# Attention value product: key tails moved and stacked by DMA, loads in pieces, and a new order of the work

## The chip, the cores and the metric

One core of a Trainium2 chip runs the whole program. The metric is device time in microseconds (us), the median of the runs. TensorE (PE, with its weight loads shown as PEld), VectorE (DVE), ScalarE (ACT), GpSimd (POOL) and SyncE (SP, which here only issues DMAs) each run one queue of instructions in order and wait for each other by semaphores.

## What is computed

Cross attention followed by a soft mixture of experts. Two batches of 1024 rows attend with 16 heads of width 64 to a context of 154 rows; a head pair is 128 columns wide.

```python
x = x + attention(layernorm(x), ctx, ctx, mask)      # q = x Wq + bq, k = ctx Wk + bk, v = ctx Wv + bv
    s0 = where(mask, NEG, q k^T / sqrt(64)); p = softmax(s0)     # per head: 1024 x 154
    out = (p v) Wo + bo
x = x + ffn(layernorm(x))                            # 16 experts with 64 slots each
    se = layernorm(slot_embeds) * scale
    logits = x se^T                                  # 2048 x 1024
    dispatch = softmax(logits, over rows); combine = softmax(logits, over slots)
    slots = dispatch^T x
    eout = (gelu(slots Wg + bg) * (slots Wu + bu)) Wd + bd
    out = combine eout
```

## The kernel before, in words

**Two halves of every operand.** Each fp32 operand of a matrix product is split into a high half (rounded to fp32r, made by ACT) and a low half (the rest, made by DVE or POOL). A product of two operands takes three passes: high by high, high by low, low by high (`PASSES`).

**The attention loop.** The 2048 rows are 8 groups of 256 (two tiles, j = 0 and 1), and the 8 head pairs are 4 quads of two pairs (pp = 0 and 1). A step n is one group and one quad, so there are 32 steps, four to a group. The parts of a step are `Q` (query projection), `S` (scores), `R` (normalisation of the exponentials), `T` (transposes of the probabilities), `PV` (probabilities times values), and once a group `LN`, `XN`, `xT` (first norm and its transposes) and `Y` (output projection of a finished group, 24 matmuls for each tile). The loop is pipelined: what `STEP` lists for step n is `Q` of step n+1, `S` of n, `T` of n-1, `PV` of n-2. `Y` stands in the second step of a group.

**The tails.** 154 keys are 128 and 26 more. `T` of part 0 and 1 (`prob`, L1476) transposes the first 128 keys of a pair's two heads; `T` of part 2 (`prob_t`, L1479) transposes the 26-key tails of all four heads of the quad at once, 4 x 26 = 104 columns, into 104 partitions of one PSUM bank. ACT copies it to `pT_high` (L899) and DVE makes `pT_low` (L1155). A `PV` is three passes of two matmuls on the first 128 keys (L1499) and one on the tails (L1501), nine in all, each with 256 moving columns. The tail values `vt` are laid out for that block-diagonally by 8 DMAs from `tails` (L600), 4 for each batch.

**Queues.** PE runs `prologue + attention + logits + slots + experts + combine` in that order. DVE, ACT and POOL run the same list, each event shifted by a table (`LATER_DVE`, `LATER_ACT`, `LATER_POOL`). `EARLY` places the projections of keys (`K`), values (`V`, `VT`) and the splits of the weights between the first steps. PSUM is shared: 3 banks for scores (`NS`), 2 for transposes (`NT`), 3 for all else (`NA`); a bank is free when DVE has made the low half of what was in it. SP issues the loads in the order of `LOADS`, then the placements of the keys (`kbd<-keys`, two DMAs for each of 6 pairs, L607), `vt`, the second batch of x, `Wo` (L614), and later the slot embeddings (L617).

**The end of attention.** The slot embeddings are normalised on DVE (`SA` statistics, `SB` values) during steps 17 to 30, one a step, and transposed on PE (`seT`). The second norm of the rows, `N2`, is one DVE operation (L1213) and two on POOL (L752, L753) for each of 16 tiles, into a ring `x2f` of three buffers; `x2T` (L1534) transposes it, and `L` (L1552) makes the logits of a tile. `Ya` are parts of the last group's output projection that are done before its last `PV`. The first three `N2` stand behind the last `R` on POOL.

## Time and profile before

| | us |
|---|---|
| median of 3 runs | 544.6 (543.71 to 545.14) |
| the profiled execution, its own time | 544.24 |
| its span (first to last instruction) | 542.5 |
| PE busy | 530.0, 98% |
| DVE, ACT, POOL busy | 434.1, 402.2, 303.3 |
| attention, to the first logits | about 0 to 289 |
| logits, slots, experts, combination | about 289 to 542 |

In these tables a busy PE does not show how close it is to its limit, since matmuls overlap: a matmul of 256 columns is shown with some 284 ns, while the next one starts 120 ns after it. What PE work costs is read from the distance of starts.

### The profile page before, as it was taken

Reading aid. Unit: us, or ns where it says so; the run is one execution under the profiler, and the core shown is the slowest. Engines: PE = TensorE matmul, PEld = TensorE weight load, DVE = VectorE, ACT = ScalarE, POOL = GpSimd, SP = SyncE. Lnnn points to the kernel's source line nnn. Section 1 sums busy time; section 2 is a strip of 40 time slices with the busy share of each in tenths; the row PEclk is TensorE's granted clock in tenths of the full one; section 3 lists DMA queues with packets and bytes.
Section 4 is the critical chain, followed back from the end, with each engine's and each line's share of the span. In section 5 each row is a group of like instructions: output and inputs, shape, how many; then the busy total and the mean of one; then the engine's idle time right before and its main releaser. Section 6 shows DMA issues by size and latency. Waiting matters only on the chain.

```text
span 542.5 us, 11967 instructions
## 1 busy us (share of the span) xinstructions
PE 530.0 (98%) x3896; PEld 499.8 (92%) x3896; DVE 434.1 (80%) x1305; ACT 402.2 (74%) x1098; POOL 303.3 (56%) x327
## 2 busy tenths in 40 slices
PE   6999999999999999999998999999999999999997
PEld 4889999999999999999997888999978888899997
DVE  6777878787897979899677998798699888865453
ACT  5879969596896959779564555788979889766562
POOL 6674654544545455454365768787467999910000
DMA  8635000000030000000001333150288888525551
GB/s 257 181 86 179 3 1 2 2 2 1 3 98 2 2 2 1 2 0 4 0 1 80 155 156 156 78 201 1 79 264 283 270 306 288 182 79 170 181 167 67
DMA packets 34901, 54.11 MB, mean 100 GB/s; under 512 B 3997, under 2 KB 21497, under 8 KB 34713
## 3 DMA queue, kind: packets, MB, share of 16 engines
q1 hardware_dynamic: 34841, 53.36, 29.7%
q8 instruction: 32, 0.52, 0.4%
q14 instruction: 28, 0.23, 0.1%
HBM read 40.54 MB, written 10.49 MB: 94 GB/s over the span
## 4 chain that ended last, share of the span: by engine, by line
PE 90%; ACT 4%; DMA 2%; POOL 1%; DVE 1%; issue 1%; SPq 0%; ACTq 0%; DVEq 0%
PE ps L1461 9%; PE ps L1585 9%; PE ps L1357 9%; PE ps L1369 8%; PE ps L1610 8%; PE ps L1499 8%; PE ps L1439 7%; PE ps L1552 7%; PE ps L1476 5%; PE ps L1632 4%; PE ps L1501 4%; PE ps L1644 3%; DMA wvo_raw<-in_L_xattn_Wo_dram 2%; ACT expo L885 1%; PE ps L1615 1%; PE ps L1622 1%
## 5 line engine op out<-in xcount | busy, mean ns | idle before, releaser
L885 ACT ACTIVATE expo<-expo,nmin 128x154 f32<-128x154 f32 x256 | 106.2, 423 | 5.3 <-DVE nmin L1135 4.8
L1135 DVE CUSTOM_DVE_ANT_0 expo<-ps,maskb 128x154 f32<-128x154 f32 x256 | 69.1, 312 | 11.9 <-PE ps L1461 11.9
L723 POOL TENSOR_TENSOR prob_t<-expo,prec 128x104 f32<-128x104 f32 x64 | 23.1, 360 | 89.3 <-DVE prec L1146 89.1
L726 POOL TENSOR_TENSOR prob<-expo,prec 128x512 f32<-128x512 f32 x64 | 66.8, 1043 | 0.0
L1461 PE MATMUL ps<-kbd,qT_high 128*128 128x308 f32 x256 | 61.1, 323 | 0.0
L1155 DVE TENSOR_TENSOR pT_low<-ps,pT_high 128x512 fp32r<-128x512 f32 (+1 forms) x96 | 57.2, 596 | 4.1 <-ACT pT_high L899 3.9
L788 POOL TENSOR_TENSOR w_gu_low<-w_raw,w_gu_high 128x1024 fp32r<-128x1024 f32 x17 | 50.3, 2966 | 16.2 <-ACT w_gu_high L835 16.1
L899 ACT CAST pT_high<-ps 128x512 fp32r<-128x512 f32 (+1 forms) x96 | 49.1, 513 | 10.8 <-PE ps L1476 8.1
L803 ACT ACTIVATE oT_high<-ps,bqv_c 128x256 fp32r<-128x256 f32 x64 | 29.8, 466 | 34.8 <-PE ps L1501 34.7
L885 ACT ACTIVATION_READ_ACCUMULATOR expo<-expo,nmin 128x1 f32 x256 | 50.3, 196 | 0.0
L1461 PEld LDWEIGHTS ps<-kbd,qT_high 128*128 128x128 f32 x256 | 39.8, 190 | 0.2
L1461 PE MATMUL ps<-kbd,qT_low 128*128 128x308 f32 x128 | 39.0, 304 | 0.0
L1476 PE MATMUL ps<-ident,prob 128*128 128x128 f32 x256 | 38.5, 273 | 0.1
L1369 PE MATMUL ps<-wvo_high,oT_high 128*128 128x256 f32 x128 | 37.0, 289 | 0.0
L1501 PE MATMUL ps<-pT_high,vt 104*128 104x256 f32 x128 | 36.3, 284 | 0.0
L1369 PE MATMUL ps<-wvo_high,oT_low 128*128 128x256 f32 x128 | 36.2, 283 | 0.0
L1369 PE MATMUL ps<-wvo_low,oT_high 128*128 128x256 f32 x128 | 36.0, 281 | 0.0
L1357 PE MATMUL ps<-eo_high,comb 128*128 128x256 f32 x256 | 34.6, 287 | 0.4 <-issue 0.4
L1032 DVE SCALAR_TENSOR_TENSOR oT_low<-ps,bqv_c,oT_high 128x256 fp32r<-128x256 f32 x64 | 30.3, 474 | 5.3 <-ACT oT_high L803 4.5
L922 ACT COPY lsb<-ps 128x512 f32<-128x512 f32 x32 | 17.2, 589 | 22.3 <-PE ps L1552 22.3
L1006 ACT CAST comb<-ps 128x512 fp32r<-128x512 f32 x32 | 17.2, 590 | 21.3 <-PE ps L1644 21.3
L1032 DVE SCALAR_TENSOR_TENSOR qT_low<-ps,bqv_c,qT_high 128x256 fp32r<-128x256 f32 x64 | 29.9, 468 | 3.7 <-ACT qT_high L803 3.6
(241 smaller groups left out, 1762.7 us busy)
## 6 DMA issues: line engine op xcount, KB each, us to landing
logits_dram<-lsb SPq DMA_DIRECT2D x16, 512.0 KB, 2.6
w_raw<-in_L_ffn_Wg_dram SPq DMA_DIRECT2D x16, 512.0 KB, 4.0
w_raw<-in_L_ffn_Wu_dram SPq DMA_DIRECT2D x16, 512.0 KB, 4.5
w_raw<-in_L_ffn_Wd_dram SPq DMA_DIRECT2D x16, 512.0 KB, 4.5
lraw<-logits_dram SPq DMA_DIRECT2D x13, 512.0 KB, 3.8
out_dram<-gate SPq DMA_DIRECT2D x16, 128.0 KB, 2.2
kbd<-keys SPq DMA_DIRECT2D x12, 154.0 KB, 2.8
wvo_raw<-in_L_xattn_Wv_dram SPq DMA_DIRECT2D x2, 512.0 KB, 7.0
```

The lines of the kernel that those rows point to most:

```text
L726: pool.tensor_tensor(prob[:, n % 2, :, heads, :], expo[:, n % 2, pp, :, :, 0:P], prec[:, n % 2, pp].unsqueeze(3).to_broadcast([P, 2, 2, P] ...
L788: pool.tensor_tensor(low, w_raw[:, i % RAW].rearrange("p (k n) -> p k n", k=KD if w == 0 else FT), high, ALU.subtract).then_inc(low_made(e ...
L885: ins = act.activation(row, row, ACT.Exp, scale=-1.0, bias=nmin[:, n % 2, pp, j, h:h + 1], accum_out=psums[:, n % 2, pp, j, h:h + 1])
L899: act.copy(pT[0][0:rows, n % 2, 2 * t:2 * t + tiles], ps[0:rows, NS + k % NT, 0:tiles * 2 * P].rearrange("p (t n) -> p t n", t=tiles))\
L1032: dve.scalar_tensor_tensor(out=dst, in0=src, scalar=bias, in1=high, op0=ALU.add, op1=ALU.subtract)\
L1135: ins = dve.tensor_tensor_reduce(out=expo[:, n % 2, pp, j, h, :], in0=ps[:, s % NS, h * SK:(h + 1) * SK], in1=maskb[:, (2 * (n // QUADS) + ...
L1155: dve.tensor_tensor(pT[1][0:rows, n % 2, 2 * t:2 * t + tiles], ps[0:rows, NS + k % NT, 0:tiles * 2 * P].rearrange("p (t n) -> p t n", t=ti ...
L1357: ins = pe.matmul(dst[:, 0:D], combT[s][:, i % 2, t], eo[m][:, i // TB, t], start=(first and r == 0 and t == parts[0]), stop=(last and r = ...
L1369: ins = pe.matmul(dst, oT[s][:, p, j * P:(j + 1) * P], wo[m][:, p], start=(first and p == 0 and r == 0), stop=(last and p == PAIRS - 1 and ...
L1461: ins = pe.matmul(dst, qT[s][:, n % 2, pp, j * P:(j + 1) * P], kbd[:, b, m, p, :], start=(r == 0), stop=(r == 2))
L1476: ins = pe.transpose(ps[:, NS + k % NT, (2 * h + j) * P:(2 * h + j + 1) * P], prob[:, n % 2, j, 2 * t + h, 0:P], ident[:])
L1501: ins = pe.matmul(dst[:, 0:2 * P], vt[:, b, s, q, pp * P:(pp + 1) * P], pT[m][0:T4, n % 2, 4], start=False, stop=(r == 2))
```

## The change

**Tails.** `prob_t` holds each pair's two tails (52 columns) in a field of 64, padded with zeros, so that part 2 of `T` transposes 128 columns and pair 0's tails land in partitions 0 to 51, pair 1's in 64 to 115. ACT and DVE write the high and low halves to `tT_high` and `tT_low`, which have one buffer. Then SP issues four DMAs of 64 partitions by 1 KB for each step, from `tT` to `tS`: for each pair the high half goes into one half of the partitions, the low half into the other. `vt` holds the tail values twice, once in each half. One matmul with the stacked `tS` then does high and low together, so a `PV` has 3 x 2 + 2 = 8 matmuls; the two tail matmuls stand at its end and wait for the DMAs (`d_tt`). ACT's copy of a step's tails waits for the DMAs of the step before.

**SP's queue.** Its DMAs follow the order of the program: keys, `vt` of batch 0 (4 DMAs, of 26 partitions by 16 pieces of 256 bytes, where there were 8 pieces), then four tail DMAs a step, and behind each step's tails up to three pieces of the loads: `Wo` in four, `vt` of batch 1 in two pairs, the second batch of x in four, gains, and later the slot embeddings by tile. `tails` lies in the memory of the second batch of x. The first loads change their order: the first piece of Wk is ahead of x.

**Orders.** A new `STEP`, new tables of shifts, a new prologue and new `EARLY`: the last tail projection `VT` 1 now stands right ahead of part 2 of `T` of step 0. `Wo` is split in four pieces at step 4. `NORM_AT` gives the places of `SA` and `SB` (steps 17, 18, 19, 21, 22, 23, 25, 26, 27, 29, and three in 30, ahead of the table's shifts). The second norm has four buffers (`NX`), and its first four tiles stand at place 6 of the end of attention, where three stood at place 19. `Ya` parts are moved.

```diff
+FOURTHS = tuple((at, at + 256) for at in range(0, 1024, 256))
 DIRECT = (0, 1)
-PIECES = {WK: QUARTERS, WQ: QUARTERS, WV: HALVES, WO: HALVES}
+PIECES = {WK: QUARTERS, WQ: QUARTERS, WV: HALVES, WO: FOURTHS}
...
-    ("x",), ("split", WK, 0), ("split", WQ, 0), ("bias",), ("split", WK, 1), ("split", WV, 1),
-    ("split", WK, 2), ("split", WV, 0), ("mask",), ("split", WQ, 1), ("split", WQ, 2),
+    ("split", WK, 0), ("x",), ("split", WQ, 0), ("bias",), ("split", WQ, 1), ("split", WV, 1), ("mask",),
+    ("split", WK, 2), ("split", WQ, 2), ("split", WV, 0), ("split", WK, 1),
...
+    ("S", 0, 0, 0): [("Q", 0, 1), ("K", 2), ("split", WQ, 1)], ("S", 1, 0, 1): [("V", 1, 0)],
+    ("S", 1, 1, 1): [("V", 0, 1), ("V", 1, 1)], ("T", 3, 2): [("split", WO, 0), ("split", WO, 1), ("split", WO, 2), ("split", WO, 3)],
+    ("T", 0, 2): [("K", 7), ("K", 6), ("VT", 1), ("zeros", 2)], ("S", 1, 0, 0): [("XB", 0)],
...
-STEP = "R1 S00 S01 PV0 T0 LN R0 PV1 Q0 XN S10 Q1 T2 S11 T1 xT0 Y0 xT1 Y1"
+STEP = "R1 S00 S01 Q0 PV0 T2 S10 R0 LN Q1 S11 T0 XN xT0 xT1 PV1 T1 Y0 Y1"
...
-N2_AT = 19
-YA_AT = {(0, 0): 26, (1, 0): 26, (0, 1): 28, (1, 1): 29}
...
+N2_AT = 6
+YA_AT = {(0, 0): 25, (1, 0): 31, (0, 1): 35, (1, 1): 31}
 A_LATE = 3
+NORM_AT = (18, 19, 20, 22, 23, 24, 26, 27, 28, 30, 31, 31, 31)
+NX = 4
+PIECES_A_MOVE = {"K": 0, "VT": 0, "Q": 0, "T": 3}
...
-        head.insert(head.index(("S", GROUPS // B * QUADS + 1 + k + (k >= ST // 2), 0, 0)), ev)
-    tail = tail[:N2_AT] + [("N2", 0), ("N2", 1), ("N2", 2)] + tail[N2_AT:] + [("x2T", 0)]
+        head.insert(head.index(("Q", NORM_AT[k], 1)), ev)
+    tail = tail[:N2_AT] + [("N2", i) for i in range(NX)] + tail[N2_AT:] + [("x2T", 0)]
...
+    second_at = -(-nc.sbuf_base // 32) * 32 + 4 * TB * D
     x1 = sb(top, "x1", [P, TILES, D])
+    tails = nc.alloc_sbuf_tensor_at("tails", [B * TAIL, 2, DM], F32R, offset=second_at)
...
-    vt = sb(att, "vt", [T4, B, 2, QUADS, 4 * DH], F32R)
+    vt = sb(att, "vt", [P, B, 2, PAIRS, P], F32R)
...
-    prob_t = sb(att, "prob_t", [P, 2, 2, 4, TAIL])
+    prob_t = sb(att, "prob_t", [P, 2, 2, 2, DH])
...
-    pT = halves(loop, "pT", [P, 2, 5, 2 * P])
+    pT = halves(loop, "pT", [P, 2, 4, 2 * P])
+    tT = halves(loop, "tT", [P, 2 * P])
+    tS = sb(loop, "tS", [P, 2, 2, 2 * P], F32R)
...
+        def place_values(b, a):
+
+            for twice in range(2):
+                at = twice * DH + a * TAIL
+                sp.dma_start(vt[at:at + TAIL, b, :, :, a * DH:(a + 1) * DH]
+                             .rearrange("p s q d -> p (s q) d").bitcast(F32),
+                             tails[b * TAIL:(b + 1) * TAIL].rearrange("p s (q a d) -> p (s q) a d", a=2, d=DH)
+                             [:, :, a, :].bitcast(F32)).then_inc(d_tails[b], 16)
+
+        def place_keys(ev):
+
             wait_used(sp, ev)
+            for h in range(2):
+                at = slice(h * DH, (h + 1) * DH)
+                sp.dma_start(kbd[at, :, :, ev[1], h * SK:(h + 1) * SK].rearrange("p b s k -> p (b s) k").bitcast(F32),
+                             keys[at, placed_no[ev] % NK].rearrange("p b s k -> p (b s) k").bitcast(F32)).then_inc(d_keys[ev], 16)
+
+        def place_tails(ev):
+
+            for half, done in ((0, t_high), (1, t_free)):
+                sp.wait_ge(done, t_no[ev] + 1)
+                for pp in range(2):
+                    to = pp ^ half
+                    sp.dma_start(tS[to * DH:(to + 1) * DH, ev[1] % 2, pp].bitcast(F32), tT[half][pp * DH:(pp + 1) * DH].bitcast(F32))\
+                        .then_inc(d_tt, 16)
...
+            elif kind == "wo":
+                at = slice(2 * k, 2 * k + 2)
+                sp.dma_start(wo[2][:, at], Wo.rearrange("(k p) n -> p k n", p=P)[:, at]).then_inc(d_w[WO][0], 16)
...
+        rest, wo_asked = [], False
+        for at, ev in enumerate(moves):
             if ev == LAST_VT:
-
-                sp.wait_ge(vt_zeros, 2)
-                for b in range(B):
-                    for a in range(4):
-                        sp.dma_start(vt[a * TAIL:(a + 1) * TAIL, b, :, :, a * DH:(a + 1) * DH]
-                                     .rearrange("p s q d -> p (s q) d").bitcast(F32),
-                                     tails[b * TAIL:(b + 1) * TAIL].rearrange("p s (q a d) -> p (s q) a d", a=4, d=DH)
-                                     [:, :, a, :].bitcast(F32)).then_inc(d_tails[b], 16)
+                wait_used(sp, LAST_VT)
+                sp.wait_ge(vt_zeros, 3)
+                for a in range(2):
+                    place_values(0, a)
+            elif ev[0] == "K":
+                place_keys(ev)
             else:
-                for h in range(2):
-                    at = slice(h * DH, (h + 1) * DH)
-                    sp.dma_start(kbd[at, :, :, ev[1], h * SK:(h + 1) * SK].rearrange("p b s k -> p (b s) k").bitcast(F32),
-                                 keys[at, placed_no[ev] % NK].rearrange("p b s k -> p (b s) k").bitcast(F32)).then_inc(d_keys[ev], 16)
-        sp.dma_start(x1[:, TB:TILES], x_t[:, 1]).then_inc(d_x_second, 16)
-        sp.dma_start(gain[:], norm_g.unsqueeze(0).to_broadcast([P, D])).then_inc(d_gain, 16)
-        sp.dma_start(shift[:], norm_b.unsqueeze(0).to_broadcast([P, D])).then_inc(d_gain, 16)
-
-        wait_done(sp, LAST_V)
-        sp.dma_start(wo[2], Wo.rearrange("(k p) n -> p k n", p=P)).then_inc(d_w[WO][0], 16)
-
-        sp.wait_ge(s_full, s_no[("S", GROUPS // B * QUADS - 1, 1, 1)] + 1)
-        sp.dma_start(se[:], slot_embeds.rearrange("(t e) s d -> (e s) t d", e=P // SLOTS)).then_inc(d_se, 16)
-        sp.dma_start(sg_b[:], slot_g.unsqueeze(0).to_broadcast([P, D])).then_inc(d_se, 16)
-        sp.dma_start(sb_b[:], slot_b.unsqueeze(0).to_broadcast([P, D])).then_inc(d_se, 16)
-        sp.dma_start(sc_b[:], scale.unsqueeze(0).to_broadcast([P, 1])).then_inc(d_se, 16)
+                place_tails(ev)
+            if before_ffn.index(ev) > before_ffn.index(LAST_V) and not wo_asked:
+
+                wait_done(sp, LAST_V)
+                wo_asked = True
+                rest = [("wo", k) for k in range(PAIRS // 2)] + [("vt", a) for a in range(2)] + \
+                    [("x", k) for k in range(TB // 2)] + [("gain", 0)]
+            if at == se_at:
+
+                sp.wait_ge(s_full, s_no[("S", GROUPS // B * QUADS - 1, 1, 1)] + 1)
+                rest = [("se", None)] + [("se", t) for t in range(ST)] + rest
+            for piece in rest[:PIECES_A_MOVE[ev[0]]]:
+                load_part(*piece)
+            rest = rest[PIECES_A_MOVE[ev[0]]:]
...
+                if t == 2 and n:
+
+                    act.wait_ge(d_tt, 64 * n)
+                dst, tiles = (pT[0][:, n % 2, 2 * t:2 * t + 2], 2) if t < 2 else (tT[0][:].unsqueeze(1), 1)
+                act.copy(dst, ps[:, NS + k % NT, 0:tiles * 2 * P].rearrange("p (t n) -> p t n", t=tiles))\
                     .then_inc(t_high, 1)
...
-                        ins = pe.transpose(ps[0:T4, NS + k % NT, j * P:(j + 1) * P],
-                                           prob_t[:, n % 2, j].rearrange("p h k -> p (h k)"), ident[:])
+                        ins = pe.transpose(ps[:, NS + k % NT, j * P:(j + 1) * P],
+                                           prob_t[:, n % 2, j].rearrange("p q k -> p (q k)"), ident[:])
...
-                both = max(t_no["T", n, pp], t_no["T", n, 2]) + 1
-                pe.wait_ge(t_high, both)
+                k = t_no["T", n, pp] + 1
+                pe.wait_ge(t_high, k)
...
-                    ins = pe.matmul(dst[:, 0:2 * P], vt[:, b, s, q, pp * P:(pp + 1) * P], pT[m][0:T4, n % 2, 4],
-                                    start=False, stop=(r == 2))
+                pe.wait_ge(d_tt, 64 * (n + 1))
+                for s in range(2):
+                    ins = pe.matmul(dst[:, 0:2 * P], vt[:, b, s, p, :], tS[:, n % 2, pp], start=False, stop=(s == 1))```

PE, the first `PV` (step 0, pair 0) and what stands ahead of it, before:

```order
L1461 MATMUL ps<-kbd,qT_high 128x308
L1461 MATMUL ps<-kbd,qT_low 128x308 [waits acc_free]
L1499 MATMUL ps<-pT_high,vm_high 128x256 [waits vm_zeros,d_tails0,acc_free,t_high]
L1499 MATMUL ps<-pT_high,vm_high 128x256
L1501 MATMUL ps<-pT_high,vt 128x256
L1499 MATMUL ps<-pT_high,vm_low 128x256 x2
L1501 MATMUL ps<-pT_high,vt 128x256
L1499 MATMUL ps<-pT_low,vm_high 128x256 [waits t_free]
L1499 MATMUL ps<-pT_low,vm_high 128x256
L1501 MATMUL ps<-pT_low,vt 128x256
```

The same place now, with the transposes of the next step's tails behind it:

```order
L1503 MATMUL ps<-xT_low,wkq_high 128x256 [waits acc_free]
L1503 MATMUL ps<-xT_low,wkq_high 128x256
L1565 MATMUL ps<-pT_high,vm_high 128x256 [waits vm_zeros,d_tails0,acc_free,t_high]
L1565 MATMUL ps<-pT_high,vm_high 128x256
L1565 MATMUL ps<-pT_high,vm_low 128x256 x2
L1565 MATMUL ps<-pT_low,vm_high 128x256 [waits t_free]
L1565 MATMUL ps<-pT_low,vm_high 128x256
L1569 MATMUL ps<-tS,vt 128x256 [waits d_tt]
L1569 MATMUL ps<-tS,vt 128x256
L1545 MATMUL ps<-ident,prob_t 128x128 [waits tail_ready,t_free]
```

The three tail matmuls inside the block became two at its end, behind a wait for a DMA.

SP, from the last keys to Wo, before (118 rows in all):

```order
L607 DMA kbd<-keys 64x4x154 [waits acc_free]
L607 DMA kbd<-keys 64x4x154
L600 DMA vt<-tails 26x8x64 [waits vt_zeros,acc_free]
L600 DMA vt<-tails 26x8x64 x7
L609 DMA x<-in_x_dram 128x2048
L610 DMA gain<-in_L_ffn_norm_g_dram 128x256
L611 DMA shift<-in_L_ffn_norm_b_dram 128x256
L614 DMA wvo_raw<-in_L_xattn_Wo_dram 128x8x256 [waits acc_full]
```

And now (253 rows in all):

```order
L622 DMA kbd<-keys 64x4x154
L612 DMA vt<-tails 26x16x64 [waits vt_zeros,acc_free]
L612 DMA vt<-tails 26x16x64 x3
L631 DMA tS<-tT_high 64x256 [waits t_high]
L631 DMA tS<-tT_high 64x256
L631 DMA tS<-tT_low 64x256 [waits t_free]
L631 DMA tS<-tT_low 64x256
```

The tails of step 0 are queued behind four placements of `vt`; those of step 1 follow, and then three pieces of Wo.

POOL at the end of attention, before: the last two `R` (steps 31, pair 0 and 1) and the first `N2`.

```order
L723 TENSOR_TENSOR prob_t<-expo,prec 128x2x52 [waits t_full,recip_ready]
L726 TENSOR_TENSOR prob<-expo,prec 128x2x256
L752 TENSOR_TENSOR x2f<-x2f,gain 128x256 [waits d_gain,x2_centered]
L753 TENSOR_TENSOR x2f<-x2f,shift 128x256 [waits pool_step]
L752 TENSOR_TENSOR x2f<-x2f,gain 128x256 [waits x2_centered]
```

And now:

```order
L788 TENSOR_TENSOR prob<-expo,prec 128x2x256
L814 TENSOR_TENSOR x2f<-x2f,gain 128x256 [waits d_gain,x2_centered]
L815 TENSOR_TENSOR x2f<-x2f,shift 128x256 [waits pool_step]
L814 TENSOR_TENSOR x2f<-x2f,gain 128x256 [waits x2_centered]
L815 TENSOR_TENSOR x2f<-x2f,shift 128x256 [waits pool_step]
L814 TENSOR_TENSOR x2f<-x2f,gain 128x256 [waits x2_centered]
L815 TENSOR_TENSOR x2f<-x2f,shift 128x256 [waits pool_step]
L814 TENSOR_TENSOR x2f<-x2f,gain 128x256 [waits x2_centered]
L815 TENSOR_TENSOR x2f<-x2f,shift 128x256 [waits pool_step]
L785 TENSOR_TENSOR prob_t<-expo,prec 128x2x52 [waits t_full,recip_ready]
L788 TENSOR_TENSOR prob<-expo,prec 128x2x256
```

Four `N2` now stand ahead of both `R` of the last step.

## Rows read from the trace of the kernel before

**Rows 1.** The page, busy us, share of the span and instructions

```profile
PE 530.0 (98%) x3896; PEld 499.8 (92%) x3896; DVE 434.1 (80%) x1305; ACT 402.2 (74%) x1098; POOL 303.3 (56%) x327
```

**Rows 2.** Busy time by stretch; columns as in its first line

```profile
core 0: us, PE busy (x) PEld busy (x) DVE busy (x) ACT busy (x) POOL busy (x), PEclk, DMA share, GB/s
42.00:54.00 12.00, 11.23 (x91) 10.96 (x90) 9.01 (x38) 10.98 (x40) 5.57 (x8) 1.00 0.58 189
54.00:66.10 12.10, 11.81 (x98) 11.59 (x97) 10.30 (x47) 12.10 (x46) 9.06 (x10) 1.00 0.01 3
97.80:129.60 31.80, 31.80 (x263) 31.80 (x262) 26.16 (x115) 25.19 (x94) 15.35 (x26) 1.00 0.01 2
225.00:256.70 31.70, 31.70 (x262) 31.68 (x261) 28.78 (x125) 25.20 (x94) 14.88 (x25) 1.00 0.01 2
```

**Rows 3.** The chain of waits: start us, us, engine, line, count

```profile
34.42 2.79 PE ps L1417 x12
...
42.10 9.52 DMA wvo_raw<-in_L_xattn_Wo_dram
...
66.13 5.75 PE ps L1369 x48
...
75.33 0.72 PE ps L1439 x6
...
78.70 0.85 PE ps L1461 x6
...
97.85 5.76 PE ps L1369 x48
...
256.67 5.76 PE ps L1369 x48
...
262.43 0.85 PE ps L1461 x6
```

**Rows 4.** Timeline of PE in one step: start us, us, engine, line, operation

```profile
72.56 0.40 PE L1499 MATMUL ps<-pT_high,vm_high 128*128 128x256 f32 x2
72.80 0.29 PE L1501 MATMUL ps<-pT_high,vt 104*128 104x256 f32 x1
...
73.64 0.60 PE L1476 MATMUL ps<-ident,prob 128*128 128x128 f32 x4
74.00 0.48 PE L1499 MATMUL ps<-pT_high,vm_high 128*128 128x256 f32 x2
```

**Rows 5.** Groups by line and form: busy us, mean ns, idle before

```profile
L1155 DVE TENSOR_TENSOR pT_low<-ps,pT_high 104x256 fp32r<-104x256 f32 x32 | 13.3, 416 | 2.9 <-ACT pT_high L899 2.9
...
L899 ACT CAST pT_high<-ps 104x256 fp32r<-104x256 f32 x32 | 11.9, 371 | 2.6 <-PE ps L1479 2.6
```

**Rows 6.** SP's own queue: DMA issues in time, and us each row

```profile
33.38 7.16 SPq L600 DMA_DIRECT2D vt<-tails  x8
...
485.20 0.36 SPq L658 DMA_DIRECT2D out_dram<-gate  x1
```

**Rows 7.** SP's issues by tile: duration min/median/max, and time to landing

```profile
L607 SPq DMA_DIRECT2D kbd<-keys x12: 590/610/1367, 17.9 to 31.0; - x12
...
DMA to landing us min/median/max: 2.6/2.8/3.3
```

**Rows 8.** The page's DMA issues: count, KB each, us to landing

```profile
out_dram<-gate SPq DMA_DIRECT2D x16, 128.0 KB, 2.2
```

**Rows 9.** Timeline of PE at the start and behind attention

```profile
31.72 0.45 PE L1461 MATMUL ps<-kbd,qT_high 128*128 128x308 f32 x2
...
288.67 0.71 PE L1552 MATMUL ps<-wkq_high,x2T_high 128*128 128x512 f32 x2
...
295.81 0.41 PE L1534 MATMUL ps<-ident,x2f 128*128 128x128 f32 x2 [1.11 <-POOL x2f L753]
```

**Rows 10.** Timeline of POOL at the end of attention

```profile
279.33 0.73 POOL L752 TENSOR_TENSOR x2f<-x2f,gain 128x256 f32<-128x256 f32 x1
280.14 0.74 POOL L753 TENSOR_TENSOR x2f<-x2f,shift 128x256 f32<-128x256 f32 x1
```

166 lines of the change are left out of this document (91 added, 75 removed).

## The prediction

> **What bounds the kernel now.** The page first: PE is busy 98% of the span, ACT 74%, DVE 80% [rows 1]. Whether PE is at its limit shows only where one stretch is taken apart, so I read the stretches, the chain and one step.
>
> In the steady part of attention the chain goes from one output projection to the next, at 66.13 and 97.85 us, and six such distances reach 256.67 [rows 3]: 31.7 us a group, with PE busy for all of it [rows 2]. ACT is busy for 25.2 of it and DVE for 26.2, in the second batch for 28.8 [rows 2]. So PE is the bound there, and a matmul taken out is worth its pitch. The pitch is read from starts: a `PV` block runs from 72.56 to 73.64, 1.08 us for nine matmuls, 0.12 each [rows 4]. It is not the 0.29 us that a record shows.
>
> In two other places PE is not alone. From 42 to 66 us ACT is busy for 23.1 of 24.1 us, PE for 23.0 [rows 2]: both are at their limit, and 9.5 us of the chain are the DMA of Wo [rows 3]. At the end of attention PE waits for POOL: 1.11 us ahead of the fourth `x2T`, at 295.81 [rows 9].
>
> **The change, part by part.** The sum is made against the profiled execution, 544.24 us, of which 542.5 are the span. The median of the runs is 0.36 above it, and I add that at the end.
>
> *One matmul fewer in each PV.* 64 blocks by 0.12 us are 7.7 us. 8 of these blocks lie ahead of the first projection at 66.13, 48 between there and step 30 (262.43), 8 behind [rows 3]: 0.96, 5.76 and 0.96 us. The transposes are as many as before. What each share brings depends on what else is late in its stretch.
>
> *The new way of the tails, in the steady part.* Behind `T` part 2 come ACT's copy (0.37 us), DVE's low half (0.42) [rows 5] and four DMA issues. The low half is done while the two high DMAs are issued, so that the last issue starts three issues behind the copy. A single issue takes between 0.36 us (an output row [rows 6]) and 0.61 (keys moved inside SBUF [rows 7]). From issue to landing it is 2.2 us (128 KB to DRAM [rows 8]) to 2.8 (154 KB inside SBUF [rows 7]); I put the 64 KB of a tail nearer to the small one, 2.3, and an issue at 0.45. The chain is 0.37 + 3 x 0.45 + 2.3 = 4.0 us, with the bounds 3.7 and 5.0, plus what ACT and DVE have queued. Against that stands PE's own work up to the tail matmuls of the next step: four `S` at 0.42 (half of 0.85), two `Q` at 0.72 [rows 3], two `T` at 0.36 [rows 4], one `PV` of 0.96 and six matmuls of the next: 5.5 us, in the step with the projection 11.3. The DMAs are hidden with 0.5 to 1.8 us to spare for queueing.
>
> The Trainium skill, "DMA: Bandwidth & Descriptors", section "Anatomy of one DMA", puts a DMA at some 2.0 us plus bytes over 436 GB/s, for its GpSimd path; for 64 KB that is 2.15 us as an estimate, where the keys' row says 2.8. By the page the chain is 3.9 us and its upper bound falls to 4.3; by the keys' row it is 4.5. Both fit into 5.5, but only the page leaves room for a DVE that is a microsecond late.
>
> DVE does get late: in the step behind a projection it has the second `Y` (add and statistics, about 1 us), two `xT` halves and, in batch 1, a norm. ACT comes near its limit too. A group without its projection was 31.7 - 5.76 = 26.0 us of PE work and will be 25.0, and ACT has 25.2 [rows 2]. I take 0.15 us a group for the first three groups and 0.25 for the others in waits, about 1.0 in all (between 0 and 2.8). This part gives 5.76 - 1.0 = **4.8 us**.
>
> *The start.* SP's queue is in order, and the tails of step 0 stand behind four placements of `vt`. Before, the second tail projection ended on PE at 31.72 [rows 9] and SP issued the first `vt` at 33.38 [rows 6], 1.66 later. One of these took 7.16 / 8 = 0.9 us with its gap [rows 6]. They now have twice as many pieces: between 0.83 and 1.66 each; I take 1.0, near the old price, since the 256 pieces of a keys' placement cost 0.61 [rows 7] and the 208 of a `vt` more: the number of pieces alone doesn't set it. Then come three issues and a landing: 1.66 + 4.0 + 1.35 + 2.3 = 9.3 us, with the bounds 8.3 and 12.9. PE meanwhile has `T` 0.2, four `S` 1.7, two `Q` 1.44, two `V` (2.79 for the pair [rows 3]), two `T` 0.72 and six matmuls 0.72: 7.6 us. So the first `PV` waits **1.7 us** (0.7 to 5.3). Behind it on PE is everything, the transposes of step 1's tails first, so it is a full loss. Against it stand the first weights, one issue earlier (-0.4), and Wo, which arrives in pieces and is wanted two steps later: of PE's 0.77 us of idle time between 42 and 54 [rows 2] I take back 0.5. Of the 0.96 us of removed matmuls I take nothing, since ACT, with no less work, is full there. The start costs **0.8 us** (-1.9 to +4.4). The `vt` of batch 1 takes SP some 4 us within a step of over 6: hidden, at 1.66 each not quite.
>
> *The end.* Step 30 began at 262.43 and the logits at 288.67 [rows 3, 9]. 0.96 us of matmuls go. But four `N2` at 1.5 us each (279.33 to 280.84 was one [rows 10]: two operations of 0.73) now stand on POOL ahead of the last two `R`, 6 us in which no probabilities are made; and DVE carries two `SB`, the four `N2` and a late `Y` in steps 30 and 31. PE's work between the first `S` of step 31 and its tail transposes is about 7.7 us. POOL, which can't start the norms before DVE's first one, needs 6.0 for them and 1.8 for `R`. I give back 0.7 of the 0.96: **0.3 us** gained (from 1.0 gained to 1.5 lost). The last tails' DMAs have 4.8 us of other PE work above them, chain 4.0.
>
> *Four buffers.* The fourth norm is made before the logits, so the 1.11 us at 295.81 [rows 9] go. The next to come late would be the fifth; it gets its buffer with the first `x2T`, and PE needs 3 us for each tile. **1.1 us** gained.
>
> *Free.* Zeroing of `prob_t`, the second norm of x in pieces, and slot embeddings by tile: they lie in stretches where their queues idle and are wanted steps later.
>
> Sum: +0.8 - 4.8 - 0.3 - 1.1 = -5.4, so 538.8 for an execution like the profiled one and **539.2 us** as a median.
>
> **The rivals.**
>
> *All hidden.* The orders were made for these DMAs, the first `PV` doesn't wait and every stretch is PE's: 7.7 + 1.1 + 0.9 for the start = 9.7, 534.9 us. For it: PE lost almost nothing in the steady part before. Against it: ACT's 23.1 of 24.1 us.
>
> *The start, the end and the steady part at their upper bounds.* `vt` at 1.66 an issue and landings at 2.8 make +4.4 at the start, the end loses 1.5, and the waits of the steady part leave 3.0 of its 5.76: 4.4 + 1.5 - 3.0 - 1.1 = +1.8, 546.4 us. More likely only one of them is dear: 541.5 to 544.
>
> *Slower: the tails miss their slot in each step.* The chain is at its bound of 5.0 and DVE's and ACT's queues add over half a microsecond, so that the tail matmul waits in every step without a projection. From 66.13 on there are 18 such steps. From 0.33 us a step the gain of 5.9 outside the start is gone; at 0.8 us it is 14.4, against -5.4: 553 us. For it: SP, ACT and DVE take turns four times a step, and the copy has one buffer. Against it: in the middle of the bounds it has 1.5 us to spare.
>
> *The matmuls are not fewer.* The order of instructions shows two tail matmuls in each block, so this one falls.
>
> **Chances.** My forecast, 537 to 541.3: 0.50. All hidden, 533.5 to 537: 0.20. Start or end dearer, 541.3 to 546: 0.18, half of it below 543. Missed slots, above 546: 0.12. A measurement of this kernel can tell about 0.3%, 1.6 us, from no change. So faster by more than that: 0.50 + 0.20 + 0.09 = 0.79; the same: 0.08; slower: 0.13. The range takes the forecast and most of the two beside it: 534.5 to 544.5.
>
> **What would show it.** Distances between projections of 30.8 to 31.1 us instead of 31.7; above 31.4 the slots are missed, and the waits of the tail matmul will name a DMA of `tS`. A wait of 1 to 3 us ahead of the very first tail matmul, near 40 us, with `tS<-tT` behind it; SP's `vt` issues at 1.0 us. The projection at 66.13 near 67. From step 30 to the logits some 26 us, with POOL's norms ahead of a late `prob_t`. No wait at the fourth `x2T`. The forecast is wrong if ACT, now even with PE in steps without a projection, makes PE wait for its copies throughout, or if the first `PV` waits 4 us.

## The result, and the profile after

The changed kernel takes **548.7 us** (median of 4 executions, 547.9 to 550.0) against 544.6 before: a ratio of 1.0078 with a 95% interval of 1.0057 to 1.0098. It was forecast at 539.2, between 534.5 and 544.5. So the forecast was wrong in sign: slower by 4.1 us instead of faster by 5.4. Measured again beside later experiments, it took 547.5 (6 executions, 545.9 to 550.4).

The profiled execution took 548.52 us with a span of 546.7. Its page, which answers [rows 1]:

```profile
span 546.7 us, 11989 instructions
PE 525.5 (96%) x3832; PEld 492.2 (90%) x3832; DVE 435.9 (80%) x1306; ACT 404.0 (74%) x1100; POOL 305.0 (56%) x329
PE 79%; DVE 8%; DMA 5%; ACT 4%; issue 2%; SPq 1%; ACTq 0%; DVEq 0%
```

PE has the 64 matmuls less, but its share falls from 98% to 96%, and in the last line, the chain that ended last, from 90% to 79%. DVE and DMA now hold 13% of it. The same line of before:

```profile
PE 90%; ACT 4%; DMA 2%; POOL 1%; DVE 1%; issue 1%; SPq 0%; ACTq 0%; DVEq 0%
```

The six distances between projections stand in the chain, start and duration in us [rows 3]:

```profile
72.41 5.67 PE ps L1433 x48
103.02 5.67 PE ps L1433 x48
133.61 5.69 PE ps L1433 x48
164.38 5.69 PE ps L1433 x48
195.72 5.67 PE ps L1433 x48
228.07 5.69 PE ps L1433 x48
259.46 5.68 PE ps L1433 x48
```

Between the first and the last lie 187.05 us, where it was 190.54: **3.5 us gained**. But the first comes 6.3 us later (72.41 against 66.13). PE's own rows name the waits ahead of it, in brackets with what ended them:

```profile
17.41 0.76 PE L1503 MATMUL ps<-xT_high,wkq_high 128*128 128x256 f32 x2 [2.17 <-DVE xT_low L1093]
45.62 0.50 PE L1569 MATMUL ps<-tS,vt 128*128 128x256 f32 x2 [1.02 <-DMA tS<-tT_low]
63.67 0.66 PE L1542 MATMUL ps<-ident,prob 128*128 128x128 f32 x4 [1.57 <-DVE tT_low L1220]
68.29 0.50 PE L1569 MATMUL ps<-tS,vt 128*128 128x256 f32 x2 [1.70 <-DMA tS<-tT_low]
```

The second of them is the wait that the prediction named (1.7 us; with a gap of 0.27 ahead of the same block it is 1.3 instead). The other three it did not have.

The end runs from step 30's first score to the first logits, and then to the rest of the logits. The first row is of the trace of before, the others are of the changed kernel:

```profile
262.27 0.45 PE L1461 MATMUL ps<-kbd,qT_high 128*128 128x308 f32 x2
264.98 0.44 PE L1525 MATMUL ps<-kbd,qT_high 128*128 128x308 f32 x2
293.28 0.71 PE L1618 MATMUL ps<-wkq_high,x2T_high 128*128 128x512 f32 x2
299.17 0.38 PE L1600 MATMUL ps<-ident,x2f 128*128 128x128 f32 x2
```

28.3 us; the same two starts lie 26.4 us apart in the trace of before (262.27 and 288.67 [rows 9]): **1.9 us lost**. In the other profiles with this end unedited it took 27.6 to 28.7 us (27.6 in the repetition of this very kernel), so that a single one of them tells the loss only to about a microsecond. The fourth `x2T`, at 299.17, has no wait any more [rows 9]: **1.2 us gained** up to the experts. The experts took 0.9 us more.

### The profile page after: what moved, and what is told of

It reads as the page before. It is cut to its first block, busy times and chain, and to the rows that moved or that the text cites. A ratio compares the mean times of both kernels' runs of the same rounds, so it can differ in the third digit from the quotient of the medians.

```text
span 546.7 us, 11989 instructions
## 1 busy us (share of the span) xinstructions
PE 525.5 (96%) x3832; PEld 492.2 (90%) x3832; DVE 435.9 (80%) x1306; ACT 404.0 (74%) x1100; POOL 305.0 (56%) x329
## 4 chain that ended last, share of the span: by engine, by line
PE 79%; DVE 8%; DMA 5%; ACT 4%; issue 2%; SPq 1%; ACTq 0%; DVEq 0%
PE ps L1651 8%; PE ps L1421 8%; PE ps L1618 8%; PE ps L1433 8%; PE ps L1525 8%; PE ps L1503 7%; PE ps L1565 6%; PE ps L1676 5%; PE ps L1542 4%; PE ps L1710 3%; PE ps L1569 3%; PE ps L1698 2%; PE ps L1464 2%; PE ps L1481 2%; DMA tS<-tT_low 2%
## 5 line engine op out<-in xcount | busy, mean ns | idle before, releaser
L946 ACT ACTIVATE expo<-expo,nmin 128x154 f32<-128x154 f32 x256 | 106.2, 420 | 41.2 <-DVE nmin L1199 41.2
L785 POOL TENSOR_TENSOR prob_t<-expo,prec 128x104 f32<-128x104 f32 x64 | 23.4, 365 | 95.1 <-DVE prec L1210 93.2
L788 POOL TENSOR_TENSOR prob<-expo,prec 128x512 f32<-128x512 f32 x64 | 67.8, 1059 | 0.0
L1525 PE MATMUL ps<-kbd,qT_high 128*128 128x308 f32 x256 | 60.9, 322 | 0.0
L850 POOL TENSOR_TENSOR w_gu_low<-w_raw,w_gu_high 128x1024 fp32r<-128x1024 f32 x17 | 49.4, 2906 | 18.0 <-ACT w_gu_high L896 17.9
L946 ACT ACTIVATION_READ_ACCUMULATOR expo<-expo,nmin 128x1 f32 x256 | 49.4, 193 | 0.0
L1220 DVE TENSOR_TENSOR pT_low<-ps,pT_high 128x512 fp32r<-128x512 f32 x64 | 43.5, 679 | 0.0
L1525 PEld LDWEIGHTS ps<-kbd,qT_high 128*128 128x128 f32 x256 | 39.8, 189 | 0.2
L1542 PE MATMUL ps<-ident,prob 128*128 128x128 f32 x256 | 38.2, 272 | 1.6 <-DVE tT_low L1220 1.6
L1525 PE MATMUL ps<-kbd,qT_low 128*128 128x308 f32 x128 | 38.9, 304 | 0.0
L1433 PE MATMUL ps<-wvo_high,oT_high 128*128 128x256 f32 x128 | 36.8, 288 | 1.0 <-DVE oT_low L1095 1.0
L963 ACT CAST pT_high<-ps 128x512 fp32r<-128x512 f32 x64 | 37.1, 581 | 0.4 <-PE ps L1542 0.3
L1433 PE MATMUL ps<-wvo_low,oT_high 128*128 128x256 f32 x128 | 36.0, 281 | 0.0
L1433 PE MATMUL ps<-wvo_high,oT_low 128*128 128x256 f32 x128 | 36.0, 281 | 0.0
L1106 DVE TENSOR_TENSOR w_gu_low<-w_raw,w_gu_high 128x1024 fp32r<-128x1024 f32 x14 | 30.1, 2148 | 5.3 <-ACT w_gu_high L896 5.2
L1542 PEld LDWEIGHTS ps<-ident,prob 128*128 128x128 f32 x256 | 30.6, 140 | 1.8 <-DVE tT_low L1220 1.8
## 6 DMA issues: line engine op xcount, KB each, us to landing
out_dram<-gate SPq DMA_DIRECT2D x16, 128.0 KB, 2.2
```

What stands on the lines that cost most here:

```text
L788: pool.tensor_tensor(prob[:, n % 2, :, heads, :], expo[:, n % 2, pp, :, :, 0:P], prec[:, n % 2, pp].unsqueeze(3).to_broadcast([P, 2, 2, P] ...
L850: pool.tensor_tensor(low, w_raw[:, i % RAW].rearrange("p (k n) -> p k n", k=KD if w == 0 else FT), high, ALU.subtract).then_inc(low_made(e ...
L946: ins = act.activation(row, row, ACT.Exp, scale=-1.0, bias=nmin[:, n % 2, pp, j, h:h + 1], accum_out=psums[:, n % 2, pp, j, h:h + 1])
L1220: dve.tensor_tensor(dst, ps[:, NS + k % NT, 0:tiles * 2 * P].rearrange("p (t n) -> p t n", t=tiles), high, ALU.subtract).then_inc(t_free, 1)
L1433: ins = pe.matmul(dst, oT[s][:, p, j * P:(j + 1) * P], wo[m][:, p], start=(first and p == 0 and r == 0), stop=(last and p == PAIRS - 1 and ...
L1525: ins = pe.matmul(dst, qT[s][:, n % 2, pp, j * P:(j + 1) * P], kbd[:, b, m, p, :], start=(r == 0), stop=(r == 2))
```

## The experiments

The theory: the stacked tails pay as computed, and what is lost lies in the new orders (loads and copies at the start, Wo, norms). The rival: the moves of the tails by DMA are what costs. Where "best" stands beside a median, it is the lowest execution: those of this family lie further apart than those of the kernel before (543.1 to 546.1 in all but one of 96, one at 548.5), and the last section of this part is about that. A span is that of the one profiled execution.

### Are the moves hidden?

*No moves at all.* The tail matmuls read `tT` where ACT and DVE left it, in two buffers; the result is another one.

```diff
-                    sp.dma_start(tS[to * DH:(to + 1) * DH, ev[1] % 2, pp] ...
+            sp.wait_ge(t_free, t_no[ev] + 1)
...
-                    ins = pe.matmul(..., tS[:, n % 2, pp], ...)
+                    ins = pe.matmul(..., tT[s][:, n % 2], ...)
```

> The changed kernel without the four moves of the tails in each step: the tail matmuls read the transposed tails where the copies left them (two buffers), so the output is not the reference's; PE, ACT, DVE and POOL do the same number of instructions. Order theory (the moves are hidden but for the first): the six distances between projections stay at 30.6 in batch 0 and 31.3 to 32.4 in batch 1, the waits ahead of the tail matmuls at 44 and 68 us go (1.2 and 1.9 us), and one at the end (0.6); 3 to 3.5 us faster than the changed kernel. Rival (the moves are what costs, by late buffers for ACT's copy and by late tails): distances in batch 1 fall to 30.7, the end gets 1.5 to 2 us shorter, in all over 5 us faster.

Measured: 543.4 us (540.7 to 547.6). Its distances between projections are 30.6 in batch 0, and 30.6, 32.4, 31.3 in batch 1, as with the moves (31.3, 32.4, 31.4) but for the first. The two waits for `tS` are gone and the first projection comes 2.8 us earlier, with the other waits in place. From step 30 to the logits it takes 27.8, within the 27.6 to 28.7 of the kernels with moves. So the moves are hidden in the steady part but for 0.7 us in one distance, and cost 2.8 us at the start; a cost at the end isn't shown. By the medians, 543.4 against 548.7 and 547.5, they cost 4.1 to 5.3 in all, more than the 3 to 3.5 of the order theory; but the rival's signs, batch 1 back at 30.7 and an end 1.5 to 2 us shorter, are absent. Batch 1 and the end are slow without the moves. And without any of them, with 64 matmuls less, this order of the work is only 0.9 us faster than the kernel before (ratio 0.9967, 0.9948 to 0.9986).

*Eight moves of half the size.*

> The changed kernel with each move of the tails issued as two of half the size, eight in a step instead of four: some 2 to 2.4 us more on SP ahead of the last landing. It measures the slack of the chain. If the slack is the 0.5 to 1.8 us of my prediction, a step without a projection gets 0.5 to 2 us longer and the distances go from 30.6 to 32.5 to 36: 12 to 35 us slower than the changed kernel. If it is larger than 2.4 us, distances stay at 30.6 and only the start (2 us) and the end (1 to 2 us) get longer: 551 to 553.

589.1 us, 40 us slower, outside both ranges and nearer to the first. SP's timeline of one step, start and duration of groups:

```profile
124.42 2.38 SPq L633 DMA_DIRECT2D tS<-tT_high  x4
126.85 2.51 SPq L633 DMA_DIRECT2D tS<-tT_low  x4
131.96 3.52 SPq L633 DMA_DIRECT2D tS<-tT_high  x4
135.53 2.52 SPq L633 DMA_DIRECT2D tS<-tT_low  x4
```

An issue costs 0.6 us for 32 KB as for 64, so the chain is about 2.5 us longer. In batch 0 a group gets 4.0 to 5.0 us longer, some 1.5 for each of its three steps without a projection (in the group that got 5.0 longer the clock fell once as well). The slack was about 2.5 - 1.5 = **1 us**, an estimate, within the 0.5 to 1.8 of the prediction. The third row shows a group of four that took 3.52 instead of 2.38: more of that below.

*The old orders around the new tails.*

```diff
-STEP = "R1 S00 S01 Q0 PV0 T2 S10 R0 LN Q1 S11 T0 XN xT0 xT1 PV1 T1 Y0 Y1"
+STEP = "R1 S00 S01 PV0 T0 LN R0 PV1 Q0 XN S10 Q1 T2 S11 T1 xT0 Y0 xT1 Y1"
...
```

> The changed kernel's way of the tails, its loads in pieces and its four buffers, but with the orders of before the change (start, loads, order of a step, shifts, second norms, early projections). In that order of a step the tail transposes come ahead of the last scores of a step, and PE has 2.4 us of work from there to the tail matmuls of the next (two scores 0.86, a score 0.43, transposes 0.36, six matmuls 0.72). Theory (the moves need 3.7 to 5 us behind the transposes): a wait of 1.3 to 2.6 us in each of the 24 steps without a projection, 30 to 60 us slower than the changed kernel: 575 to 605. Rival (the order of a step is not what hides the moves): within 5 us of 548.7.

616.6 us: worse than expected, and groups of 38.7 to 41.4 us. Part of the excess is the clock: its mean is 0.961, and it stands at its lower level in 14 stretches behind such waits, some 21 us at the 1.5 us that a fall costs below. A row of it:

```profile
92.71 0.51 PE L1583 MATMUL ps<-tS,vt 128*128 128x256 f32 x2 [1.50 <-DMA tS<-tT_low]
```

The rival "missed slots" of the prediction looks like this. The new orders keep it away. That it is the order of a step, with `T2` early, is the likely reading, but this run undoes all orders together.

### The start

*All of it as before* (loads, order, shifts; Wo apart), twice, the second time with GpSimd's low halves in the right order:

```diff
 LOADS = [
+    ("x",), ("split", WK, 0), ("split", WQ, 0), ("bias",), ("split", WK, 1), ("split", WV, 1),
...
-LATER_POOL = {'Y1': 2.5, ("split", WQ, 1): -4}
+LATER_POOL = {'Y1': 2.5, ("K", 0): -1, ("split", WV, 0): 5}
```

> The changed kernel with the loads, the order ahead of the first scores and the table entries of that stretch as they were before the change (x first, the second piece of Wk fifth and not last, the mask's conversion behind the low halves of the keys). Order theory (the start got longer because copies wait for late loads and stand ahead of wanted ones, after which the granted clock falls): Q(0, 0), at 17.4 us in the changed kernel and 14.4 before, comes back to about 14.4 to 15, the granted clock between 15 and 20 us to 1.00, and the kernel gains 2.5 to 4 us against the changed one: 544.7 to 546. Rival (the stacked tails set the start: placements of the values and the moves of step 0 end at the same time whatever comes ahead): the gain turns into a longer wait ahead of the first tail matmul, 1.6 us now and over 3 then, and the kernel stays at 548 to 549.

> The undoing of the start again (loads and order ahead of the first scores as before the change), this time with GpSimd (POOL) making the low half of Wq's second piece ahead of that of Wv, as it did before. In the first try PE stood still for 6.4 us at 19.2 us waiting for that half, since POOL had the 1024 columns of Wv first. Order theory: no such wait, the first PV at 39 to 41 us (43.6 in the changed kernel, 39.2 before), granted clock 1.00 between 15 and 25 us, and the span falls from 546.7 to 543 to 544.5. Rival (the stacked tails' placements set the first PV): the first scores come 2 to 4 us earlier, and the wait ahead of the first tail matmul grows from 1.2 us by as much; span 546 to 547.

The first was a failure of my own making: 555.8 us. Without the shift of `("split", WV, 0)`, POOL makes the low half of Wv's 1024 columns ahead of that of Wq:

```profile
25.60 0.77 PE L1503 MATMUL ps<-xT_high,wkq_high 128*128 128x256 f32 x2 [6.39 <-POOL wkq_low L760]
```

The second took 547.0 us (best 545.0). `Q(0, 0)` came at 14.7 as expected, but PE then stood idle for 1.7 us behind a half of Wq and 1.1 behind one of the values, and the first PV came at 42.6: neither prediction can be told from it.

*More warming in the gap.*

```diff
-    ("zeros", 1), ("warm", 5), ("cTt",), ...
+    ("zeros", 1), ("warm", 12), ("cTt",), ...
```

> The changed kernel with 12 instead of 5 warming matmuls in the gap ahead of Q(0, 0), nothing else. In the changed kernel PE is idle for 2.2 us there and the granted clock then stands at 0.50 from 18 to 20 us. Clock theory (that halved stretch costs about 1.8 us and comes from the gap): clock 1.00 from 16 to 22, first scores at 20.8 us instead of 22.6, span 544.6 to 545.2, a time of 546.5 to 547 in all runs. Rival (the clock falls for what the DMAs and other engines do in that stretch, or the matmuls delay Q by as much as they give): time unchanged at 548 to 549, or some runs with the fall and some without.

545.3 us (best 544.6), span 543.5, 2.2 to 3.4 us below the unedited kernel. The columns of the next rows are stretch, length, PE's busy time, the granted clock (1.00 is 2.4 GHz, 0.50 is 1.2), the DMAs' share and their GB/s. In the changed kernel:

```profile
15.00:18.00 3.00, 0.83 (x5) 0.89 0.65 255
18.00:21.00 3.00, 3.00 (x13) 0.54 0.00 0
```

Behind the gap of 2.2 us the clock is near its lower level: the query and the key block behind it take twice their time. From `Q(0, 0)` to the first score it is 5.2 us, 3.6 with the warming: **the fall costs 1.5 us**. With nothing of it left, the first projection of this run stands at 69.91:

```profile
69.91 5.69 PE ps L1433 x48
```

That is **3.8 us later than before**, and this is the run against which the others are read. Of the 2.5 us that it is ahead of the changed kernel here, 1.5 are the clock; the rest is a DMA that landed sooner (under "why executions differ"). In three of its ten executions the mean clock was below 1.00 nevertheless (548.2 to 549.6 us), which is the second half of the rival: a fall in some executions and not in others.

*Wo asked for at once, and its halves behind step 3's tails.*

```diff
-    ("T", 3, 2): [("split", WO, 0), ("split", WO, 1), ("split", WO, 2), ("split", WO, 3)],
+    ("T", 3, 2): [("split", WO, 0)], ("S", 4, 1, 0): [("split", WO, 1)],
+    ("Q", 5, 1): [("split", WO, 2)], ("S", 4, 1, 1): [("split", WO, 3)],
...
+            take = PIECES_A_MOVE[ev[0]] + (rest[:1] == [("wo", 0)])
```

> The changed kernel with the fourth piece of Wo asked for together with the first three, and the halves of pieces two to four taken from ahead of step 3's tail transposes to behind them, one at a time. Order theory: the two waits at 63.7 (1.6 us) and 68.3 (1.7 us) go, the first projection comes at about 69 instead of 72.4, the kernel gains 3 to 3.5 us: 545.2 to 545.7. Rival (copy engine ACT is at its limit in this stretch whatever the order, as its 23.1 of 24.1 us before say): the waits move elsewhere between 50 and 72 us, the gain is below 1 us: 547.7 to 548.7.

545.7 us (best 543.5), span 543.0. PE's idle time between 50 and 72 us falls from 3.3 to 1.5 (1.1 before the change):

```profile
64.11 0.50 PE L1571 MATMUL ps<-tS,vt 128*128 128x256 f32 x2 [0.29 <-DMA tS<-tT_low]
65.50 0.41 PE L1547 MATMUL ps<-ident,prob_t 128*128 128x128 f32 x2 [0.89 <-DVE pT_low L1222]
```

Time and first projection (69.3) are what the theory wanted. But e9_warm, with Wo as in the changed kernel, reaches nearly the same (545.3 us, 69.9) with 2.0 us of idle time there, and h1_both below, with this edit, again has a wait of 2.5 us ahead of the same tail matmul. Most of the difference is the landing of one move, not the order. The order of Wo's halves is worth about 0.5 us (2.0 against 1.5, one execution each), and a part of the waits moves on to the next copy, since ACT is full there, as the rival had it.

*The second tail projection earlier.*

```diff
-... ("S", 1, 0, 1): [("V", 1, 0)],
+... ("S", 1, 0, 1): [("VT", 1), ("V", 1, 0)],
...
```

> The changed kernel with 12 warming matmuls (as e9_warm, which had 1.2 us of wait ahead of the first tail matmul, at 44 us) and the second tail projection VT 1 two scores earlier, ahead of V(1, 0), so that SP can place the values sooner. Theory (SP's order sets the first PV: four placements of 0.9 us each behind VT 1, then the moves of step 0): the placements start 2 to 4 us earlier, the wait ahead of the first tail matmul goes (1.2 us), the first projection comes at 68.5 instead of 69.7. Rival (what is late there is the transposed tails themselves, by ACT's and DVE's copies): the placements start earlier and the wait stays at 1.0 to 1.2 us.

548.9 us, 3.6 slower than e9_warm: PE now waits where the halves of Wv aren't ready (1.18, 1.29 and 1.57 us between 30 and 39 us), and at 32 us the clock falls once, 1.5 us of it. The wait ahead of the first tail matmul shrinks to 0.2 us, but the first PV itself comes 5.1 us later (47.5), so this doesn't tell whether the placements set it: the question stays open in this form.

*The start, mended.* The start of before with Wq's second piece early in all queues, and Wo as above.

> The changed kernel with the start of before the change, but Wq's second piece loaded and halved early (POOL has it ahead of Wv's), the halves of the last pieces of Wq and Wv on ACT as in the changed kernel, and Wo as in e2_wo. Theory (order of loads and copies): Q(0, 0) at 14.6, first scores at 18.2, no wait over 0.5 us until the first PV, which comes at 39 to 40 us (42.4 in e9_warm); first projection at 66 to 67 us (69.7), span 540 to 541.5. Rival (the placements of the values set it): the wait ahead of the first tail matmul grows from 1.2 to 3 or 4 us, first projection at 68.5 to 69.5, span 542.5 to 543.5.

Span **540.6**, best 542.4, the median of only four 547.6. First projection at 68.1, 2.0 us later than before instead of 3.8, though the theory wanted 66 to 67. Of these 2.0, 1.3 are the wait behind the placements, which did not grow: so orders cost 1.8 us here, and that wait 1.3. Its other three executions took 547.1 to 550.2 us. One wait is left ahead of the first PV:

```profile
20.44 0.48 PE L1505 MATMUL ps<-xT_high,wkq_high 128*128 128x256 f32 x2 [1.13 <-POOL wkq_low L762]
```

### The norms and the end

*Second norms late* (`N2_AT = 20` for 6), and *slot norms one in a step*:

> The changed kernel with the four second norms behind the last probabilities, as before the change, instead of ahead of the scores of step 31. Order theory: from step 30 to the logits it takes 26.2 to 26.8 us instead of 28.1, and the kernel gains 1.3 to 2 us: 546.7 to 547.4. Rival (the end is longer because three slot norms and the moves of the tails meet there, not for the second norms): no more than 0.5 us gained, 548.2 to 548.7; or a loss, if the first x2T now comes late.

> The changed kernel with the slot norms one in each step from 17 to 30 (but 21), as before the change, so that steps with a projection have one too and the last step has one instead of three. Order theory (their new places cost something): the projections of batch 1 stand 30.8 apart instead of 31.3 to 32.4, and the kernel gains 1 to 2.5 us: 546.2 to 547.7. Rival (the norms cost what they cost, since DVE is full in batch 1 with a shorter step): within 0.5 us of 548.7. The intention of the change (norms in steps with a projection delay it): 0.5 to 2 us slower, 549.2 to 550.7.

547.8 us and 548.9: by the medians, neither gains. In the stretches, step 30 to the logits takes 27.5 us with the second norms late, and 27.1 with the slot norms spread, but batch 1 pays about 1 us for it (31.2, 32.9, 31.8 between projections, against 31.3, 32.4, 31.4). With the end unedited it is 27.6 to 28.7, so the first is no gain clear of that spread, and the second at most 0.5 us. In the first, DVE still has its four operations ahead of the last low half:

```profile
279.85 3.00 DVE L1277 TENSOR_SCALAR x2f<-x,mv,rstd 128x256 f32<-128x256 f32 x4
282.77 0.41 DVE L1220 TENSOR_TENSOR tT_low<-ps,tT_high 128x256 fp32r<-128x256 f32 x1
283.24 0.66 PE L1542 MATMUL ps<-ident,prob 128*128 128x128 f32 x4 [1.30 <-DVE tT_low L1220]
```

*A third order for the end*, with these behind it too and the early projection later:

> The changed kernel with 12 warming matmuls (e9_warm, 543.5 us of span, 28.7 us from step 30 to the logits) and another order at the end: the second norms behind the last probabilities on GpSimd and behind the last low halves of the transposes on DVE, the last two slot norms on DVE only ahead of where their transposes need them, the first early projection three events later. Theory (orders at the end cost the 2 to 2.5 us): 26.2 to 26.9 us from step 30 to the logits, span 541.3 to 541.8, a time of about 543.2. Rival (the stacked tails cost it: one more hop by DMA behind the last probabilities): 28 us or more, with a wait at the tail matmuls of steps 30 and 31 that grows by as much.

546.9 us (best 544.7), 28.7 us from step 30 to the logits: nothing gained, by neither theory as put. The early projection had filled the time in which PE waits for the last probabilities, and I had moved it away; that is a reading, since this run has three changes in one. But both edits of the end together (h1_both, and h2_four_more with the same end) give 26.6 and 26.5 us, against 26.4 before and 27.6 to 28.7 with the end unedited:

```profile
265.13 0.44 PE L1527 MATMUL ps<-kbd,qT_high 128*128 128x308 f32 x2
291.69 0.71 PE L1620 MATMUL ps<-wkq_high,x2T_high 128*128 128x512 f32 x2
```

So the end's loss is one of orders. It isn't all gained, though: the three distances of batch 1 add up to 96.6 and 95.8 us in these two, and to 94.6 to 95.2 where the slot norms stay at their new places. Some 1 us of the 1 to 2 goes back there.

*The slot norms where they were.*

> e9_warm with the slot norms ahead of the first scores of steps 18 to 30, one in each, with the shifts on DVE that they had before the change (theirs were 17 to 20 and 22 to 30; 17 is too early, since the slot embeddings now arrive in pieces). In the changed kernel DVE's second operation of such a norm takes up to 1.15 us (0.48 the others) where GpSimd's product of probabilities runs beside it, and sb_b 1.13 us against 0.35 before. Theory (the place of the norms against GpSimd's operations costs, not their number in a step): all of these at 0.48 and 0.35, the three distances of batch 1 (31.2, 32.3, 31.2) fall to 30.7 to 31.2, the span is 1 to 2.5 us shorter than e9_warm's 543.5. Rival (DVE is full in batch 1): the same durations, and distances whose sum stays within 0.5 us of 94.7.

557.7 us. `sb_b` is at 0.35 us and the second operation of each norm at 0.48, as the theory had it (one first operation took 1.37), but its distances in batch 1 are 35.1, 36.8 and 36.0. The shifts are counted in events. One norm fewer ahead of the first score put `R(21, 1)`, DVE's reciprocal, ahead of `S(22, 0, 0)`, and so in each step:

```profile
182.46 0.18 DVE L1210 RECIPROCAL prec<-psums 128x4 f32<-128x4 f32 x1 [0.97 <-ACT expo L946]
183.22 0.41 PE L1545 MATMUL ps<-ident,prob_t 128*128 128x128 f32 x2 [0.46 <-POOL prob_t L785]
```

DVE stands behind ACT's exponentials with PE's next scores unread. A cost by place, 12 us against e9_warm, where I was looking for 1 to 2.5. Whether the norms' own places cost anything can't be read from it.

### Four buffers alone

Four buffers in the kernel of before, nothing else:

> The kernel of before the change with four buffers for the second norm instead of three, nothing else (the fourth norm stands beside the other three). Theory: the wait of 1.11 us ahead of the fourth x2T goes and nothing else gets late, 543.2 to 543.6 against 544.6. Rival (the fourth norm on GpSimd ahead of the last copies costs as much as it brings): 544.3 to 545.

544.63 us, 544.61 before (ratio 0.9995, 0.9979 to 1.0011): the rival. From the first logits to the experts it is 1.3 us shorter, from step 30 to the logits 1.2 longer; the first of these waits is new, the second stands in the trace of before too (0.65 us at 286.83):

```profile
283.02 0.36 PE L1370 MATMUL ps<-wvo_high,oT_high 128*128 128x256 f32 x1 [0.96 <-DVE oT_low L1033]
288.63 0.44 PE L1535 MATMUL ps<-ident,x2f 128*128 128x128 f32 x2 [0.64 <-DVE oT_low L1033]
```

### All together, and why executions differ

> The changed kernel with the four edits that each shortened their stretch: the start of g2_start, Wo of e2_wo, the slot norms of e4_norms, the second norms of e3_n2_late. g2_start had 540.6 us of span. If the stretches add up (end 0.8 shorter by e3, norms 0.4 by e4): 539.2 to 540 us of span, a best time of 541 to 541.8, 0.5% below the 544.3 of before. Rival: the end is bound by the last step's probabilities, so that e3 and e4 took away the same wait: 540 to 540.6 of span.

545.0 us (542.2 to 548.7, 12 executions), against 544.0 before: ratio 1.0023, 1.0001 to 1.0045. Its best is 1.3 us below the best of before (543.5), its median above. The span of its profiled execution is 544.3 us, with a fall of the clock, so both of its expectations (540.6 and less) were missed. No kernel of this study that computes the same result has a median clearly below the one of before. (g3_all, the mended start with g1_end's end, was expected at 539 to 541.5 us and had 547.8, with a best of 544.0.)

> The changed kernel, unedited. If the fall of the clock in its start is a matter of chance (its relatives without an edit there had it in some executions and not in others): some of its executions at 546.3 to 547 us, the others at 548 to 550. If it always falls: all at 547.8 or more.

547.5 us: both kinds of executions (545.9 to 547.9 and 549.9, 550.4), so chance has a part in it. Only the one at 545.9 has a mean clock of 1.00. Its profiled execution has no fall of the clock at 18 us, but one at 67:

```profile
64.00:67.00 3.00, 0.97 (x9) 1.00 0.54 158
67.00:70.00 3.00, 3.00 (x18) 0.59 0.59 177
```

Ahead of it stands the wait of step 3's tails, and behind these moves SP issues three loads of x, 256 KB each, one of which took 1.6 us to issue:

```profile
66.55 0.50 PE L1569 MATMUL ps<-tS,vt 128*128 128x256 f32 x2 [2.03 <-DMA tS<-tT_low]
62.33 1.23 SPq L631 DMA_DIRECT2D tS<-tT_low  x2
63.66 2.63 SPq L644 DMA_DIRECT2D x<-in_x_dram  x3
```

In the chain this move, the last of step 3, lands 3.54 us after the start of its issue at 62.96; the median of all moves is 2.0. In the changed kernel's first profile it is 3.21, in h1_both 3.69:

```profile
65.03 3.21 DMA tS<-tT_low
62.96 3.54 DMA tS<-tT_low
61.81 3.69 DMA tS<-tT_low
```

This is one event and not a price of the order. 15 profiled executions have this move with the same three loads behind it (f4_old_orders has another queue there). In six of them the second load's issue, which begins after the move's, took 1.2 to 1.6 us and the move landed in 3.2 to 3.7. In the other nine that issue took 0.45 us and the move landed in 2.0 to 2.1. (In e2_wo it was the third load's issue that was long, 1.45 us; it began 0.3 us before the landing.) So what holds up SP's issue seems to hold up the move in flight as well, and ahead of step 3's tail matmul that is worth 1.2 us or more. What it is stays open.

So the profiled executions of this kernel have a gap of some 2 us at two places (17 and 66 us), a little longer in one and a little shorter in the other, and at either place the clock falls in one of them and not in the other. Each fall costs about 1.5 us. The kernel before has no gap over 1 us in these stretches.

The third place is in the experts, whose code didn't change. From their first matmul to the end it took 148.0 us in the kernel before, in e9_warm and in h3_after_again, 148.9 in the changed kernel, and 152.2 in e8_prologue_pool, where PE waits:

```profile
435.00 1.23 SPq L707 DMA_DIRECT2D w_raw<-in_L_ffn_Wu_dram  x1
455.74 0.63 PE L1688 MATMUL ps<-ident,hid 128*128 128x128 f32 x4 [2.84 <-DVE hid L1357]
```

In e9_warm the same issue took 0.53 us and there was no such wait. The 4.2 us are this wait and the fall of the clock behind it (at 457 us), 1.5. The long issue alone doesn't make it: in e2_wo the same issue took 1.0 us, and no wait of PE there was longer than 0.8.

> h1_both with four more loads of the norm's gain (128 KB each, 512 pieces in all) from DRAM, one in each of four steps, in stretches where SP has time. Theory (SP's occasional long issue comes each time that a fixed number of pieces has been queued, and whether it falls on a critical weight decides over the wait of 3 us in the expert stage): the long issue moves from the weight at 433 us to another one, at least 5 us away, and the executions of over 2 us above the best get rarer, fewer than 3 in 10. Rival (the long issue is random, or the wait comes from something else): the same share of disturbed executions as h1_both, and the long issue at the same weight.

546.9 us; a long issue (0.8 us) at the same weight, the same wait of 2.9 us in the profiled execution (h1_both's has none), and 5 of 7 executions over 2 us above its best, where h1_both has 8 of 12. The theory of a fixed number of pieces falls as I put it. What makes SP's issue long, and why weights then land later, stays open.

## Why the prediction was wrong, step by step

- **Removed matmuls and steady part (-4.8): right in kind, -3.5.** (By its own figures, three times 0.15 and three times 0.25 in waits, the term was -4.6.) In batch 0 the distances were 30.6 to 30.8, all of the 0.96 us and a little more; I had taken 0.15 off for waits. In batch 1 -0.4, +0.4 and -0.3 instead of three times -0.7. The step that failed is "0.25 for the others": it measured 0.6, 1.3 and 0.6 us. In the first of them the moves are all of it, in the other two they are not the cause (30.6, 32.4 and 31.3 us without moves). DVE's norms are the likely one, since moving them moves the distances (e4_norms), but no run shows it by itself. The rival "missed slots" was rightly put down, though by the prediction's own sign, a distance above 31.4, it would have been called: three waits of PE for a move, 3.2 us in the whole kernel, are no wait in each step. The slack of 0.5 to 1.8 us is confirmed by eight moves and none.
- **First PV (+1.7): right in kind, 1.3.** `vt` took 0.9 us an issue (1.0 assumed), a tail's move 0.6 (0.45), its landing 2.0 (2.3). The errors cancel in part.
- **The start (+0.8): wrong, +6.3.** The failing steps are the two that I credited without costing. "-0.4 for the first weights": DVE waits 1.5 us for x, now second, so that its first norm begins 1.2 us later (6.79 against 5.63) and with it the low halves of `cT`. The order of the copies ahead of `Q(0, 0)`, which I didn't cost at all, put the mask's conversion ahead of the low halves of x and opened the gap of 2.2 us, behind which the clock fell. `Q(0, 0)` stands at 17.4 there, at 14.7 and 15.0 with the old orders (e8_prologue_pool, g2_start); no run tells x's part from that of the copies. And "-0.5 for Wo in pieces": the last piece, behind step 2's moves, landed at 59.2, and three halves stand on ACT ahead of the copy of step 3's tails; PE then waited 1.6 and 1.7 us. My own row said that ACT is full there. Of the 6.3 us the runs give 1.5 to the fall of the clock (e9_warm), some 1.2 to the late landing of one move, 1.3 to the wait at the first tails and 1.8 to orders that g2_start mends; 0.5 are left unexplained. Taking all moves away brings 2.8 of the 6.3 (e6_no_moves), since that removes the wait of step 3's tails too: orders and moves share that one. (The lower bound of this term, -1.9, isn't worked out anywhere.)
- **"Free": open in one item.** The second loads of x in pieces stand behind the moves of the tails, and a move there lands in 3.2 us in the changed kernel's chain (65.03), 3.5 in the repetition. But with the same loads it landed in 2.0 us in nine other profiles. No run takes the loads away.
- **The end (-0.3): wrong, +1.9, beyond its bound of 1.5 lost** (+1.2 in the repetition, within it). The mechanism was named (norms ahead of the last probabilities); its size wasn't. I weighed GpSimd's norms against GpSimd's time alone, though three slot norms and four second ones meet on DVE in the same steps: PE is idle 0.55 us for a `qT` low half and 1.03 ahead of the first early projection. The second wait stays at 0.9 in h1_both, whose end takes 26.6 us, so these two waits are not the whole account.
- **Four buffers (-1.1): the wait went, -1.2**; that alone they bring nothing shows that this and the end's term were one account.
- **Experts (0): +0.9** in the profiled execution, 0 in the repetition.

The sum by these: +6.3 - 3.5 + 1.9 - 1.2 + 0.9 = +4.4, against 4.3 measured between the profiled executions (548.52 against 544.24). The rival nearest to it was "the upper bounds" at 546.4. It had the place of the loss (the start), but with the tails' placements as its cause; the wait behind these is 1.3 of 6.3.

## What to carry to other kernels

Cost every new order by the event that it holds up, also where the change is said to be about something else: here the named edit paid 3.5 us of its 4.8 in the steady part, and new places of loads and copies took more than that back. Where two engines are full at once, take nothing for free. A chain through a DMA queue has a slack of its own: measure it by making it longer. And before a difference of 1 to 2 us in one stretch is put down to an edit, see how far that stretch moves in kernels without the edit: here the first projection moved by 1.8 us (70.6 to 72.4) and the end by 1.1 (27.6 to 28.7).

## What the runs showed of the hardware

**DVE and GpSimd hold each other up.** The same operation on DVE takes 0.35 us alone and 1.13 beside a product of GpSimd. In the kernel before and in the changed one (the columns are minimum, median and maximum in ns, then first and last start):

```profile
L1186 DVE TENSOR_SCALAR sb_b<-sb_b,sc_b x1: 348/348/348, 200.6 to 200.6; 128x256 f32<-128x256 f32 x1
L1250 DVE TENSOR_SCALAR sb_b<-sb_b,sc_b x1: 1127/1127/1127, 207.1 to 207.1; 128x256 f32<-128x256 f32 x1
L1262 DVE SCALAR_TENSOR_TENSOR se<-se,srs,sb_b x8: 484/485/1149, 214.7 to 271.0; 128x256 f32<-128x256 f32 x8
207.02 1.09 POOL L788 TENSOR_TENSOR prob<-expo,prec 128x512 f32<-128x512 f32 x1
```

DVE's operation began at 207.13, 0.1 us behind GpSimd's, and ended 0.15 behind its end. The mask's conversion, beside a clearing by GpSimd, took 1.72 us instead of 0.79, and the clearing behind it 1.66 instead of 1.12:

```profile
13.54 1.72 DVE L1136 TENSOR_SCALAR maskb<-mask_u 128x1232 bf16<-128x1232 uint8 x1
14.66 1.66 POOL L749 MEMSET kbd<- 64x1232 f32 x1
```

The Trainium skill, "SBUF — State Buffer", section "SBUF: two separate sides", says that GpSimd and, for some forms of its operations, DVE share a pair of ports under an exclusive lock, which whichever starts first holds for its whole instruction; the rows agree.

**Half the size didn't make an issue cheaper.** SP takes 0.6 us for a move of 64 KB and for one of 32 KB, 0.9 for a placement of 26 partitions, with 208 pieces or with 416. And now and then one takes 1.0 to 2.0 us (the longest of the 128 moves in the changed kernel: 1.77), which a chain with 1 us of slack feels. Where the second load behind the last move of step 3 had such an issue, the move landed 1.2 to 1.7 us late, in six profiled executions of six.

**The clock fell behind idle times of PE, but not by their length alone.** In the profiled executions it went to 0.5 behind idle times of 2.17 us (the changed kernel, 17 us), 2.03 (h3_after_again, 66 us), 2.42 (e6_no_moves, 17 us) and 2.49 (h1_both, 65 us), and stayed at 1.00 behind 1.95 (e2_wo, 17 us), 1.74 (h3_after_again, 17 us) and 1.70 (the changed kernel, 68 us). But it also stayed at 1.00 behind 2.73 (e7_eight_moves, 17 us) and 2.12 (e3_n2_late, 67 us), and fell behind 1.89 (e1_prologue, 74 us), 1.29 (f1_vt_early, 32 us) and two of only 0.59 and 0.57 (g3_all, 63 and 65 us). So a wait of PE can cost 1.5 us more than itself, and these rows don't tell which one will.
